# Joins of 32x32 blocks and a new order of transfers in a chunk-inverse stage

## What is computed

```python
B, L, H, DK = 4, 2048, 4, 64          # batch, length, heads, head width
q, k = l2norm(q), l2norm(k)
v, kb = v * beta, k * beta
# in chunks of `chunk` rows:
T = where(tri, 0, -(kb @ k.T))        # strictly lower triangle
for i in range(1, chunk):
    T[..., i, :] += einsum('...j,...jl->...l', T[..., i, :], T)
T = T + eye(chunk)                    # = inverse of (I + strict lower part of kb k^T)
u, w = T @ v, T @ kb
for each chunk: u2 = u - w @ S;  o = q @ S + attn @ u2;  S = S + k.T @ u2
```

## Time and profile before

| | us |
|---|---|
| median of 3 runs | 2634.45 (2634.22 to 2636.96) |
| profiled execution | 2633.81 |
| its span, first to last instruction | 2632.1 |

### The profile page before, as it was taken

One profiled execution on the slowest core, in us unless ns is written; L12 is line 12 of the kernel. 1 busy time (PEld: TensorE's weight loads), 2 busy tenths in 40 slices (PEclk: granted clock), 3 DMA queues, 4 the chain that ended last, 5 costly groups with the idle time before them and its releaser, 6 DMA issues.

```text
span 2632.1 us, 39930 instructions
## 1 busy us (share of the span) xinstructions
PE 2427.5 (92%) x13580; PEld 1690.8 (64%) x13580; DVE 1657.0 (63%) x4351; ACT 1108.4 (42%) x2285; POOL 629.4 (24%) x422
## 2 busy tenths in 40 slices
PE   6799995566998999989999999999999999999998
PEld 4466664555787888845665666666666656666665
DVE  4487874449922566535666675767667676766665
ACT  2478874446663222224333424432343334234331
POOL 2145544131101111211212231222123132312210
PEclk9999998787898999989999999999999999999999
DMA  5456565878777767421201120221022022101000
GB/s 171 152 162 192 175 196 170 236 217 206 210 173 209 226 193 236 153 84 37 57 6 51 57 58 1 57 57 28 29 58 57 1 56 57 42 15 56 9 9 8
DMA packets 393199, 274.10 MB, mean 104 GB/s; under 512 B 216610, under 2 KB 350690, under 8 KB 390802
## 3 DMA queue, kind: packets, MB, share of 16 engines
q1 hardware_dynamic: 388370, 245.95, 32.9%
q0 software_dynamic: 4640, 25.73, 3.0%
HBM read 170.70 MB, written 100.93 MB: 103 GB/s over the span
## 4 chain that ended last, share of the span: by engine, by line
PE 46%; DVE 6%; issue 2%; POOL 2%; ACT 0%; DVEq 0%; ACTq 0%; POOLq 0%
PE mx_up L1960 18%; PE mx_dn L1974 17%; PE mx_m L1910 4%; DVE mx_acc L2288 2%; PE mx_m L1937 2%; POOL mx_rms L1866 2%; PE mx_m L1914 1%; PE mx_m L1951 1%; DVE hl L2171 1%; DVE hl L2160 1%; DVE mx_rms L2165 1%; PE mx_m L1930 1%; PE mx_m L1919 1%; PE mx_m L1945 1%; PE mx_m L1924 1%
## 5 line engine op out<-in xcount | busy, mean ns | idle before, releaser
L2288 DVE SCALAR_TENSOR_TENSOR mx_acc<-mx_dn,mx_comb,mx_acc 128x256 f32<-128x256 f32 x1024 | 424.4, 477 | 370.3 <-PE mx_dn L1974 367.5
L1960 PE MATMUL mx_up<-mx_h2T,mx_eup 128*128 128x512 f32 x1024 | 494.3, 606 | 0.0
L1974 PE MATMUL mx_dn<-mx_edn,mx_hs 128*128 128x256 f32 x2048 | 487.7, 381 | 0.0
L1974 PEld LDWEIGHTS mx_dn<-mx_edn,mx_hs 128*128 128x128 f32 x2048 | 385.5, 190 | 146.4 <-issue 87.9
L2062 ACT ACTIVATE mx_hs<-mx_up 128x512 f32<-128x512 f32 x320 | 190.9, 597 | 611.3 <-PE mx_up L1960 610.6
L1960 PEld LDWEIGHTS mx_up<-mx_h2T,mx_eup 128*128 128x128 f32 x1024 | 192.5, 193 | 158.7 <-issue 148.6
L666 DVE SCALAR_TENSOR_TENSOR cv_acc<-cv_pre,conv_w,cv_acc 128x512 f32<-128x512 f32 x288 | 215.6, 750 | 78.3 <-ACT cv_acc L588 71.4
L530 PE MATMUL cv_pj<-cv_hT,wqkv 128*128 128x512 f32 x384 | 181.7, 603 | 12.8 <-ACT cv_acc L588 7.8
L700 POOL TENSOR_TENSOR rn<-cv_ss,half_pow 128x8 f32 x64 | 127.5, 1992 | 13.2 <-POOL cv_ss L696 13.2
L1852 POOL TENSOR_TENSOR mx_st<-mx_tmp,root_pow 128x24 f32<-128x24 f32 x30 | 124.6, 4170 | 20.4 <-DVE mx_tmp L2114 20.4
L1974 PEld LDWEIGHTS mx_dn<-mx_sdn,mx_hs 128*128 128x128 f32 x512 | 97.3, 190 | 40.5 <-issue 30.6
(11 more groups left out here) (294 smaller groups left out, 4042.5 us busy)
## 6 DMA issues: line engine op xcount, KB each, us to landing
kqT_d<-cv_kqc SPq DMA_DIRECT2D x16, 1024.0 KB, 8.6
vf_d<-cv_vf SPq DMA_DIRECT2D x16, 1024.0 KB, 5.2
fl_toep<-taps_d SPq DMA_DIRECT2D x32, 392.0 KB, 6.9
ds_kqT<-kqT_d SPq DMA_DIRECT2D x10, 1024.0 KB, 5.7
fl_v<-vf_d SPq DMA_DIRECT2D x8, 1216.0 KB
ci_kT<-kqT_d POOLq DMA_DIRECT2D x19, 512.0 KB, 6.1
fl_d<-fl_out POOLq DMA_DIRECT2D x8, 1029.0 KB, 7.8
xin<-_attn_hidden_states_dram SPq DMA_DIRECT2D x16, 512.0 KB, 4.1
```

The costliest lines, as they stand in the source:

```text
L1960: ins = pe.matmul(up_ps[x % 2][:], lhs, h2T[i][:, k, :], start=(k == 0), stop=(k == KD - 1))
L1974: ins = pe.matmul(dn_ps[(i + n) % 2][:, j, :], hs[x % 4][:, j * P:(j + 1) * P], rhs, start=(x == 0 and j % 2 == 0) or x >= NS, stop=(x >= ...
L2288: ins = dve.scalar_tensor_tensor(out=acc[i][:, j, :], in0=dn_ps[(i + n) % 2][:, j, :], scalar=comb[i][:, j, e:e + 1], in1=acc[i][:, j, :], ...
```

## The change

In words: `low` is dropped. joined takes, per head, two matmuls of 32x32 blocks instead of one of 96x64: the block of A below the diagonal of each half (rows 32 to 63 and 96 to 127, two row groups) by the inverse block that already stands in half. The two results go to two PSUM banks, y_ps[0] and y_ps[1], and to partitions that change with x, so both banks are used by each unit. carried takes, per head, two 32x32 blocks of top (now 32 partitions, no zeros) by Y, into two column groups of x_ps; x % 2 chooses between two sets of column groups, and the wait on half_done is for the unit before the last one. keep_Y is two copies of 32 rows for one of 96. The eight transfers of a step become six, top and half have four buffers (RB = 4) for three, and four memsets remain of nine. In SyncE's step loop load_k comes ahead of load_blocks, load_blocks is for step q + 4, and put_link(q) stands ahead of it where q + 4 is the first step of a group (where load_blocks waits for T_out), behind it otherwise. Ahead of `busy` at x = 16, 32 and 48 TensorE also waits for Y_done of the unit before.

```diff
--- before.py
+++ after.py
@@ -871,7 +871,7 @@
     RA = 2 * BT
     FIRST = (0, 2 * ST, 3 * ST, ST)
     K3 = 3 * Q
-    RB = 3
+    RB = 4
     KB = 3
     with ExitStack() as ctx:
         def sb(name, shape):
@@ -892,10 +892,9 @@
         T = [sb(f"ci_T{i}", [P, 2, Q, Q]) for i in two]
         Tt = sb("ci_Tt", [P, 2, Q, Q])
         prod = [sb(f"ci_prod{i}", [P, 512]) for i in two]
-        low = [sb(f"ci_low{i}", [P, B * H, DK]) for i in range(RB)]
-        top = [sb(f"ci_top{i}", [K3, B * H, DK]) for i in range(RB)]
+        top = [sb(f"ci_top{i}", [Q, 2, B * H, Q]) for i in range(RB)]
         half = [sb(f"ci_half{i}", [P, B * H, DK]) for i in range(RB)]
-        Y = [sb(f"ci_Y{i}", [K3, H, DK]) for i in two]
+        Y = [sb(f"ci_Y{i}", [Q, 2, H, Q]) for i in two]
         link = [sb(f"ci_link{i}", [P, B, H // 2, DK]) for i in two]
         g_ps = [[psum(f"ci_gps{i}{e}") for e in two] for i in two]
         y_ps = [psum(f"ci_yps{i}") for i in two]
@@ -994,7 +993,7 @@
             def load_blocks(q):
                 i, t = q % RB, step(q)
                 if q == 0:
-                    sp.wait_ge(zero_done, 3 * RB)
+                    sp.wait_ge(zero_done, RB)
                 if q == 0:
                     sp.wait_ge(T_out[0], 32)
                 elif q % ST == 0:
@@ -1004,9 +1003,7 @@
                 block_of = lambda d, g: d[t, g].rearrange("b h r c -> r (b h) c")
                 for n in two:
                     lo, hi = slice(2 * n * Q, (2 * n + 1) * Q), slice((2 * n + 1) * Q, (2 * n + 2) * Q)
-                    own = slice(n * Q, (n + 1) * Q)
-                    sp.dma_start(low[i][hi, :, own], block_of(m.invT_d, 2 * n + 1)).then_inc(blocks_in[i], 16)
-                    sp.dma_start(top[i][lo, :, own], block_of(m.inv_d, 2 * n)).then_inc(blocks_in[i], 16)
+                    sp.dma_start(top[i][:, n], block_of(m.inv_d, 2 * n)).then_inc(blocks_in[i], 16)
                 if q >= RB:
                     sp.wait_ge(half_out[i], 16 * (q // RB))
                 for n in two:
@@ -1053,11 +1050,14 @@
                 put_diag(3 * ST + i)
             for q in range(TB):
                 put_half(q)
+                if TB + KB + q < TB + 2 * ST:
+                    load_k(TB + KB + q)
+                if (q + RB) % ST == 0:
+                    put_link(q)
                 if q + RB < TB:
                     load_blocks(q + RB)
-                if TB + KB + q < TB + 2 * ST:
-                    load_k(TB + KB + q)
-                put_link(q)
+                if (q + RB) % ST:
+                    put_link(q)
                 if q == 3 * ST + 1:
                     first_step()
             for i in range(RB):
@@ -1100,8 +1100,6 @@
             for n in range(KB, TB + KB):
                 load_k(n)
                 if n - KB < RB:
-                    pool.memset(low[n - KB][:], 0.0).then_inc(zero_done, 1)
-                    pool.memset(top[n - KB][:], 0.0).then_inc(zero_done, 1)
                     pool.memset(half[n - KB][:], 0.0).then_inc(zero_done, 1)
             init(2)
             for p in range(1, NP):
@@ -1142,25 +1140,31 @@
                 if x >= 2:
                     pe.wait_ge(Y_done, x - 1)
                 if x % BT == 0:
+                    if x:
+                        pe.wait_ge(Y_done, x)
                     busy(x, 6)
                 if b == 0:
-                    pe.wait_ge(blocks_in[q % RB], 16 * 8 * (q // RB + 1))
+                    pe.wait_ge(blocks_in[q % RB], 16 * 6 * (q // RB + 1))
                 if x % BT == 0:
                     busy(x, 8)
                 pe.wait_ge(A_done, x + 1 if x < BT else x + 1 + NT - BT if x < 3 * BT else NT)
                 for h in range(H):
-                    ins = pe.matmul(y_ps[x % 2][0:K3, h * DK:(h + 1) * DK], a[:, b, h, 0:K3],
-                                    low[q % RB][:, b * H + h, :], start=True, stop=True)
+                    for n in two:
+                        lo, hi = slice(2 * n * Q, (2 * n + 1) * Q), slice((2 * n + 1) * Q, (2 * n + 2) * Q)
+                        ins = pe.matmul(y_ps[n][x % 2 * Q:(x % 2 + 1) * Q, h * Q:(h + 1) * Q], a[hi, b, h, lo],
+                                        half[q % RB][hi, b * H + h, Q:], start=True, stop=True)
                 ins.then_inc(y_done, 1)
 
             def carried(x):
                 q, b = x // B, x % B
                 pe.wait_ge(Y_done, x + 1)
-                if x >= 1:
-                    pe.wait_ge(half_done, x)
+                if x >= 2:
+                    pe.wait_ge(half_done, x - 1)
                 for h in range(H):
-                    ins = pe.matmul(x_ps[0:DK, h * DK:(h + 1) * DK], top[q % RB][:, b * H + h, :],
-                                    Y[x % 2][:, h, :], start=True, stop=True)
+                    for n in two:
+                        r = 2 * n + x % 2
+                        ins = pe.matmul(x_ps[r * Q:(r + 1) * Q, h * Q:(h + 1) * Q], top[q % RB][:, n, b * H + h, :],
+                                        Y[x % 2][:, n, h, :], start=True, stop=True)
                 ins.then_inc(x_done, 1)
 
             def linked(x):
@@ -1209,15 +1213,18 @@
                 act.wait_ge(y_done, x + 1)
                 if x >= 2:
                     act.wait_ge(x_done, x - 1)
-                act.activation(Y[x % 2][:].rearrange("p h c -> p (h c)"), y_ps[x % 2][0:K3, 0:H * DK], ACT.Copy)\
-                    .then_inc(Y_done, 1)
+                for n in two:
+                    ins = act.activation(Y[x % 2][:, n].rearrange("p h c -> p (h c)"),
+                                         y_ps[n][x % 2 * Q:(x % 2 + 1) * Q, 0:H * Q], ACT.Copy)
+                ins.then_inc(Y_done, 1)
 
             def keep_half(x):
                 q, b = x // B, x % B
                 act.wait_ge(x_done, x + 1)
                 for n in two:
-                    src = x_ps[n * Q:(n + 1) * Q, 0:H * DK].rearrange("p (h g c) -> p h g c", h=H, g=2)
-                    ins = act.activation(half[q % RB][n * DK:n * DK + Q, b * H:(b + 1) * H, Q:], src[:, :, n, :], ACT.Copy, scale=-1.0)
+                    r = 2 * n + x % 2
+                    ins = act.activation(half[q % RB][n * DK:n * DK + Q, b * H:(b + 1) * H, Q:],
+                                         x_ps[r * Q:(r + 1) * Q, 0:H * Q].rearrange("p (h c) -> p h c", h=H), ACT.Copy, scale=-1.0)
                 ins.then_inc(half_done, 1)
 
             def keep_link(x):
```

## The result

The changed kernel takes 2627.25 us in the median of 13 runs (2622.58 to 2631.68), the kernel before 2635.63 beside it: 8.4 us less in the medians, and a ratio of 0.996 (95% interval 0.9947 to 0.9973), which is 0.4% or about 10 us. The forecast was 26.5 us less. The sign was right and the time lies in the stated range, near its slow end; the gain is about a third of the one forecast.

What follows compares the result with a forecast made beforehand. Inverses don't bound the last two groups, TensorE does; before them a hole from a late link store. Gains of 9.2 + 4.0 + 6.1 + 7.2 = 26.5 us from 2634.45 gave 2608 us, range 2596 to 2629.

Steps and rivals of the forecast that it cites:

- Part 1, the blocks: joined and carried: 0.50 us for each group of 16 small rows; TensorE needs 1.38 us a join, 2.03 with a gram.
- The rival after the row-group rule: carried's blocks don't overlap: 0.64 us, join 0.14 longer, 4 us less gain, 2612; chance 0.17 together with both groups unoverlapped.
- the floor: Small matmuls in joined and carried at least about 25 ns apart: 0.54 us a group, stage about 2.5 us longer.
- Part 2, ScalarE: Copies in the join loop: ScalarE bounds joins with a gram at 2.20 us; joins without one take 1.40.
- Part 3, the hole: TensorE's wait for a link store moves from join 8 to join 12, about 7 us; join 16 starts 9.2 us sooner.
- the sum: Gains over the join loop: 9.2 up to join 16, then 4.0, 6.1 and 7.2 for groups 1 to 3; 26.5 us.
- rival (c): Clock falls in the small-block stream of groups 1 to 3: joins 3.6 and 2.4 us, 56 us more, 2664; chance 0.11.
- "The old stream held 1.00": Argument against the clock falling in the join loop: the old stream kept the full clock for 39 and 30 us.
- The tail: After the join loop, at the block boundary: the stage's end moves all that follows by the same time.

Runs made afterwards that it cites:

- experiment 4: Changed kernel with the small matmuls of joined and carried issued three times over, same results: 2727.4 us in its one execution.
- experiment 6: Changed kernel with four link buffers for two, so the link copy need not wait for a store of two steps ago: 2620.27 us, ratio 0.9931.
- experiment 3: Kernel before, old large blocks, with four more copies of y_ps by ScalarE in each join, leaving TensorE idle gaps: 2658.64 us in its one execution.
- experiment 5: Changed kernel with one large useless matmul (identity by 128x256) ahead of linked in every join: 2642.43 us, ratio 1.0022.
- experiment 7: Changed kernel with both four link buffers and the large useless matmul in every join: 2633.11 us, ratio 0.9984.
- experiment 8: Changed kernel with four link buffers and the large useless matmul only in joins 0 to 31, those with a gram: 2630.45 us, ratio 0.9963.
- experiment 10: Changed kernel with four link buffers and the link copy of joins 32 to 63 done by VectorE: 2620.07 us, ratio 0.9916.

## Why the prediction was half right

**Part 1, the blocks: right in direction, low in effect.** I took 0.50 us for a group of 16 rows between 0.39 and 1.07. Joined and carried together took 0.53 where I had 1.00: below even twice the lower end, 0.78. A part of that is the 0.14 us of leading cost, which carried doesn't pay. The Trainium skill, TensorEngine Tiling (Array Packing), Key Properties, says that a change of tiling mode drains the engine. This trace agrees: joined and carried have the same 32x32 tiles, and their rows overlap with no gap, while from the last start of carried (655.05) to linked with its 64x64 tiles (655.17) it is 0.12 us, where the rows of carried come in pairs 0.03 apart.

The rival after the row-group rule of the Trainium skill, TensorE: Matmul & The Clock Gate, Part 3, would have needed 16 x 0.031 = 0.50 us for carried alone. The trace speaks against it: both groups together took 0.53, and with each run three times (experiment 4) the 48 rows of carried took 0.79 us (728.21 to 729.00) and the 48 of joined 0.76, 0.016 a row in both. Nor does the floor hold here that the same page of the Trainium skill, Back-to-back issue gap, gives, about 25 ns between small matmuls: float32 rows on two tiles in turn took 0.017 us at the full clock.

**Part 2, ScalarE: right where the clock was full.** At the full clock joins with a gram went at 2.2 to 2.4 us and TensorE waited for the link copy (0.53 us a join), with 2.20 forecast, and the few without one at 1.40 and 1.33 (linked at 787.73, 789.13 and 790.46), with 1.40 forecast. At the low clock TensorE was the bound, with 2.59 and 1.43 us.

**Part 3, the hole: right in kind, and a step that failed in the count.** The link copy of join 12 waited, not that of join 8. Inverse group 1 was stored at 676.5 (674.5 assumed) and link 1 landed at 692.7 (690 assumed), which makes 2.7 of the 3.1 us missing at join 16. But I took link 1 for the only late one. Three more waits of TensorE came in groups 1 to 3, of 1.79, 2.77 and 1.01 us, 5.6 in all, which the sum put at nothing. I had allowed for 1 us at join 44; by my count of 6.5 us of SyncE a step against four joins of 1.4, it was more than a possibility. Experiment 6 shows what removing the hole and these waits is worth: the last linked came 9.1 us sooner, about the 3.1 and 5.6 us together.

**The other step that failed is the clock.** The sum took 1.00 from 705 on. That it falls stood as rival (c) with a chance of 0.11, and its mechanism came true: in every group the clock fell in the stream of small blocks, with the gaps of the changed kernel and in one fall of experiment 4 nearly without them, while large blocks with such gaps held it in three groups of four (experiment 3). "The old stream held 1.00" was no evidence for a stream whose blocks are a fraction of the old size. What it cost: about 11 joins of group 1 at 2.59 for 2.20, 4.3 us; the two fills, which start at the low clock, 1.2 + 2.7; together 8 us. With the three waits (5.6), the later start of join 16 (3.1) and about 2 us that I can't assign, that is the 18.6 us between 26.5 and 7.9. So the clock and the late link stores weigh about the same.

**And its price was as wrong as its chance.** I had 3.6 and 2.4 us for a join at the low clock and so 56 us and a slower kernel. Measured: 2.59 and 1.43. The error is the same as in part 1: I scaled 0.50 us a group by 1.75, and the pair took 0.81 instead of 1.8. The two errors met, and that is luck: cheap blocks hid most of what the low clock took, and at the low clock TensorE's 1.43 fell on the 1.40 that I had from ScalarE. Apart from the waits, the joins of groups 2 and 3 came out near the forecast for another reason than the one given. That the time lies in the stated range rests on this too.

**The tail.** I let all of the stage's gain pass to the end. From the last linked to the next block it is 8.7 us for 7.2. SyncE waits there for the last stores to land; why that takes longer now is open.

## What to carry to other kernels

When matmuls are cut into smaller blocks, ask first what keeps TensorE's clock up: here the streams with 32x32 blocks lost it in every group within 13 us, and in these traces only the large useless matmuls brought it back. Look for the wait before the work: two more buffers for a small tile gave 12 us in the medians, the recoding of two of three matmul steps with a new order of transfers 8. And when a transfer queue is reordered, list every store that someone waits for, not the one that is late today.

## What was not expected of the hardware

Float32 matmuls of 32x32 on two tiles in turn issue at 0.017 us a row at 2.4 GHz and 0.025 at 1.2 GHz: half the clock costs half as much again, not twice.

TensorE can pause 1 to 3 us in the middle of the join loop's matmuls with no semaphore to wait for: 1.67, 1.06 and 1.00 us in experiment 4, 1.85 in experiment 5, 1.04 in experiment 6, 2.26, 1.05 and 1.85 in experiment 7, 1.03, 1.54 and 3.20 in experiment 8, 1.21 in experiment 10, and none over 0.6 in the changed kernel. In nine of these twelve the clock was still full, and in all nine it fell in the pause or within 1.6 us behind it. One of 0.96 us in experiment 5 (up to 720.21) did not take it.

Their cause stays open. At the longest (816.7 to 819.9 in experiment 8) the DMA view shows the data queue at 102% of the 16 engines and one 16 KB packet on the instruction queue, started inside the pause at 817.2. Late instruction loads are a candidate: in 9 of the 12 an instruction packet started within the pause or up to 1.4 us ahead of it, where about 5 would be so by chance (an estimate from 31 such packets in the 170 us of experiment 8's join loop). But in the other three none did, and in the pause of 1.05 us the 16 engines were busy for 17% only. No kernel here tests it by itself.
